# Vision tower on one core: probabilities of the first attention divided as rows, gate and value products merged, the loops of the later stages written out, the second tile's work placed sooner, and useless products on TensorE in the first microseconds

## The reference, cut to what matters

```python
x = patches(images) @ W.T + b          # 32 images, 36 patches of 768 numbers -> 256
x = concat(cls, x) + pos               # with a second class token: S = 38 rows an image
# L0 attention: 16 heads of 16, RoPE on q and k
p = softmax(where(causal, -inf, q @ k.T / 4)); x = x + (p @ v) @ Wo.T
# L0 ffn: 8 experts, the two best of each row
g = gates(top_k(x @ w_gate.T, 2)); x = x + sum_e g[:, e] * (x @ w_in[e].T @ w_out[e].T)
# L1 attention: layer norm, 16 heads, but 8 value heads; every head reads all 8 and mixes them
s = softmax(q @ k.T / 4); out = s @ v                       # (image, row, head, 8, 16)
comp = softmax(concat(qv, out) @ Ws.T + bs, over the 8); out = (comp * out).sum(over the 8)
x = x + out @ Wf.T + bf; x = x + relu(ln(x) @ Wr1.T) @ Wr2.T
# L1 ffn: ternary weights, 256 -> 1024 -> gelu -> layer norm -> 256
```

## Time and profile before

| | us |
|---|---|
| median of 3 runs | 561.5 (561.31 to 562.29) |
| the profiled execution, its own time | 560.32 |
| its span in the trace | 558.5 |
| TensorE busy in it | 506.9 |
| VectorE busy | 375.7 |
| ScalarE busy | 272.9 |
| GpSimd busy | 190.3 |

### The profile page before, as it was taken

One profiled execution on the slowest core, in us unless ns is written; L12 is line 12 of the kernel. 1 busy time (PEld: TensorE's weight loads), 2 busy tenths in 40 slices (PEclk: granted clock), 3 DMA queues, 4 the chain that ended last, 5 costly groups with the idle time before them and its releaser, 6 DMA issues.

```text
span 558.5 us, 12004 instructions
## 1 busy us (share of the span) xinstructions
PE 506.9 (91%) x3850; PEld 424.5 (76%) x3850; DVE 375.7 (67%) x943; ACT 272.9 (49%) x634; POOL 190.3 (34%) x257
## 2 busy tenths in 40 slices
PE   2969999999999887789999999999999989889996
PEld 2758878878787665567778888888888778668885
DVE  4554464555466667565997878878878787648874
ACT  3021213232331363547668777777777886434332
POOL 3320321322323311375463364364363311222230
PEclk9788899999999999999999999999999999979999
DMA  8741333243140500000000000000000000000000
GB/s 318 285 175 38 141 150 120 80 175 150 31 169 0 179 2 2 0 1 2 1 1 2 2 0 0 0 0 0 0 0 0 2 0 1 2 9 21 21 18 22
DMA packets 8685, 29.60 MB, mean 53 GB/s; under 512 B 1936, under 2 KB 3152, under 8 KB 6352
## 3 DMA queue, kind: packets, MB, share of 16 engines
q1 hardware_dynamic: 8656, 29.23, 14.4%
HBM read 27.98 MB, written 1.25 MB: 52 GB/s over the span
## 4 chain that ended last, share of the span: by engine, by line
PE 42%; DVE 5%; issue 5%; ACT 3%; POOL 1%; DVEq 1%; POOLq 0%; ACTq 0%
PE score L2051 6%; PE tb L1803 3%; PE score L1868 3%; PE bz L2081 3%; PE tb L1805 3%; PE tb L1804 3%; PE bank L1805 3%; PE bank L1804 3%; PE bank L1803 3%; PE tb L1886 2%; PE bz L2063 2%; PE bz L1817 2%; PE bz L1803 1%; DVE we_h L1433 1%; PE tb L1817 1%
## 5 line engine op out<-in xcount | busy, mean ns | idle before, releaser
L378 POOL TENSOR_TENSOR h<-h,scaled 114x256 f32 (+1 forms) x88 | 69.0, 784 | 49.3 <-ACT scaled L681 42.7
L330 POOL TENSOR_TENSOR small<-small,half 114x1 f32<-114x1 f32 x44 | 25.7, 584 | 139.4 <-DVE small L964 139.3
L547 ACT ACTIVATE p_exp<-sc,cst 114x608 f32<-114x608 f32 x66 | 48.1, 794 | 24.7 <-DVE sc L1045 24.7
L1915 PE MATMUL bz<-ebuf 128*128 128x256 f32 x256 | 58.9, 383 | 0.0
L1915 PEld LDWEIGHTS bz<-ebuf 128*128 128x128 f32 x256 | 47.8, 192 | 6.0 <-issue 0.2
L1886 PE MATMUL tb<-cst,p_exp 114*114 114x114 f32 x352 | 44.0, 266 | 9.0 <-ACT p_exp L547 3.4
L555 ACT ACTIVATE pt<-tb 114x456 f32<-114x456 f32 x66 | 34.6, 556 | 35.3 <-PE tb L1886 35.3
L2051 PE MATMUL score<-v,pt 114*114 114x137 f32 x352 | 48.9, 282 | 0.3 <-ACT o L648 0.3
L1886 PEld LDWEIGHTS tb<-cst,p_exp 114*114 114x114 f32 x352 | 35.2, 134 | 18.2 <-ACT pt L555 6.7
L681 ACT ACTIVATE scaled<-bank,gl 114x256 f32<-114x256 f32 x88 | 39.0, 473 | 17.3 <-DVE gl L1249 5.9
L2051 PEld LDWEIGHTS score<-v,pt 114*114 114x114 f32 x352 | 44.1, 178 | 2.1 <-issue 0.4
(11 more groups left out here) (216 smaller groups left out, 1338.7 us busy)
## 6 DMA issues: line engine op xcount, KB each, us to landing
ebuf<-in_w_in SPq DMA_DIRECT2D x8, 1024.0 KB, 4.8
ebuf<-in_w_out SPq DMA_DIRECT2D x8, 1024.0 KB, 6.8
x_raw<-in_x_tiles SPq DMA_DIRECT2D x11, 342.0 KB, 3.0
out<-h SPq DMA_DIRECT2D x10, 114.0 KB
raw<-in_w_a SPq DMA_DIRECT2D x4, 256.0 KB, 4.2
ebuf<-in_fc SPq DMA_DIRECT2D x1, 1024.0 KB, 5.6
ebuf<-in_proj SPq DMA_DIRECT2D x1, 1024.0 KB, 7.6
raw<-in_w_a SPq DMA_DIRECT2D x2, 384.0 KB, 5.2
```

The costliest lines, as they stand in the source:

```text
L378: gp.tensor_tensor(h[0:R, t, :], h[0:R, t, :], scaled[0:R, e % 4, :], ALU.add).then_inc(moe_acc, 1)
L547: act.activation(p_exp[0:R, :, b * S:(b + 1) * S], sc[0:R], ACT.Exp, bias=cst[0:R, CB + b:CB + b + 1], scale=SCALE).then_inc(exps, 1)
L1915: last = pe.matmul(bz[:, m * D:(m + 1) * D], ebuf[:, 0, c * D + m * P:c * D + (m + 1) * P], ebuf[:, 1, c * D:(c + 1) * D], start=(c == 0), ...
```

## The change

1. **Softmax of the first attention.** ScalarE takes the exp once, on the narrow `sc` of 608 columns. VectorE sums it over the 38 keys, takes the reciprocal of the 114 x 16 sums and multiplies `sc` by it (`a2_norm`). Three copies on ScalarE with a scale of 0 or 1 a row (`inside`) make the wide `p_exp` (`a2_wide`). The eight products with `hsum` and the wide reciprocal and product fall away, and the next `scores` waits for `xtl` instead of L1064.
2. **Products of stage C.** The gate's six passes become four, since `wc`'s two halves are taken as 16 columns for the high half of x. The products for q, k, v and the mixing, cut 512 + 152 columns before, are cut 392 + 272. The copy of the rows `qk_rows` is made in two halves, and the turns of q and k wait for both.
3. **Loops of C and D.** Both are written out in a new order on every engine, with work of stage D placed among the last turns of stage C. The loop of stage A stays. In it, half of `combine(t, 1)` now stands ahead of `a1_turn(t - 1)`.
4. **Prologue.** The second tile's patches, layer norm and products stand ahead of the preparation of the weights and of the first expert's second half.
5. **Useless products.** `warm(12)` ahead of the first tile's patches and `warm(14)` behind them multiply a matrix of ones on TensorE into a PSUM bank that is overwritten later.

```diff
+WQ = D + VW + RK
+W4 = 2 * D + W2
+C_QK, C_G, C_F, C_R1, C_R2, C_END = np.cumsum([0, DC * W4, DC * E, DC * D, DC * 2 * D, 4 * D]).tolist()
...
+            def a2_exp(n):
+                act.wait_ge(shifted, 2 * n + 2)
+                act.activation(sc[0:R], sc[0:R], ACT.Exp, scale=SCALE).then_inc(dense, 1)
+
+            def a2_wide(n, batches=range(G)):
+                act.wait_ge(scaled_rows, n + 1)
+                since(act, pt_mm, 4 * n)
+                for b in batches:
+                    act.activation(p_exp[0:R, :, b * S:(b + 1) * S], sc[0:R], ACT.Copy,
+                                   scale=inside[0:R, b:b + 1]).then_inc(exps, 1)
+
             def a2_o(t):
-                act.wait_ge(o_ready, t + 1)
+                act.wait_ge(pv0_mm, t + 1)
                 since(act, wo_mm, t)
-                act.activation(xth[1][:], y2[:], ACT.Copy).then_inc(oT_hi, 1)
+                act.activation(xth[1][:], two(score[:, 0, 0:2 * R]), ACT.Copy).then_inc(oT_hi, 1)
...
                 a1_x(t)
-                softmax_exp(t - 1)
+                a2_exp(t - 1)
+                a2_wide(t - 1)
...
-            def c2_rows(t):
-                act.wait_ge(qk1_mm, t + 1)
+            def c2_rows(t, parts):
                 since(act, qkT1_mm, 2 * t)
-                act.activation(qk_rows[0:R], tb[1][0:R, :], ACT.Copy).then_inc(qk1_out, 1)
+                if 0 in parts:
+                    act.wait_ge(qk1_mm, t + 1)
+                    act.activation(qk_rows[0:R, 0:D], tb[1][0:R, 0:D], ACT.Copy).then_inc(qk1_out, 1)
+                if 1 in parts:
+                    act.wait_ge(v1_mm, t + 1)
+                    act.activation(qk_rows[0:R, D:2 * D], tb[0][0:R, 0:D], ACT.Copy).then_inc(qk1_out, 1)
...
-            def a2_recip(t):
-                dve.wait_ge(pv0_mm, t + 1)
-                V.reciprocal(rinv0, score[:, 0, 2 * R:4 * R]).then_inc(rinv0_ready, 1)
-
-            def a2_o(t):
-                dve.wait_ge(rinv0_ready, t + 1)
-                since(dve, oT_lo, t)
-                V.tensor_tensor(y2[:], two(score[:, 0, 0:2 * R]), two(rinv0), ALU.mult).then_inc(o_ready, 1)
+            def a2_norm(n, k):
+                if k == 0:
+                    dve.wait_ge(dense, n + 1)
+                    V.tensor_reduce(psum_rows[0:R, 0], sc[0:R], AX, ALU.add).then_inc(summed, 1)
+                elif k == 1:
+                    dve.wait_ge(summed, n + 1)
+                    V.reciprocal(psum_rows[0:R, 1], psum_rows[0:R, 0]).then_inc(inverted, 1)
+                else:
+                    dve.wait_ge(inverted, n + 1)
+                    V.tensor_tensor(sc[0:R], sc[0:R], psum_rows[0:R, 1].unsqueeze(2).broadcast_to([R, H, S]),
+                                    ALU.mult).then_inc(scaled_rows, 1)
 
             def a2_lo(t):
                 dve.wait_ge(oT_hi, t + 1)
-                V.tensor_tensor(xtl[1][:], y2[:], xth[1][:].bitcast(F32), ALU.subtract).then_inc(oT_lo, 1)
+                V.tensor_tensor(xtl[1][:], two(score[:, 0, 0:2 * R]), xth[1][:].bitcast(F32), ALU.subtract).then_inc(oT_lo, 1)
...
                 softmax_max(t - 1)
                 softmax_sub(t - 1)
                 a1_x(t)
+                a2_norm(t - 1, 0)
+                a2_norm(t - 1, 1)
+                a2_norm(t - 1, 2)
                 a1_rope(t)
                 a1_pt(t - 1, (1, 3))
                 expert_lo(t)
-                a2_recip(t - 1)
-                a2_o(t - 1)
...
-            expert_lo(0)
-            prep_products()
             a1_moments(1)
-            a1_pt(0, (1, 3))
+            a2_norm(0, 0)
+            a2_norm(0, 1)
+            a2_norm(0, 2)
             a1_normed(1)
             a1_x(1)
-            a2_recip(0)
-            a2_o(0)
+            a1_pt(0, (1, 3))
+            expert_lo(0)
             a1_rope(1)
             a2_lo(0)
             a1_k(1, (0, 1))
+            prep_products()
+            a2_res(0)
+            prep_out()
+            a1_moments(2)
...
             def scores(n, causal):
                 if causal:
-                    since(pe, o_ready, n)
+                    since(pe, oT_lo, n)
...
-                            pe.matmul(score[32 * j:32 * j + 32, 0, c * R:(c + 1) * R], v0[0:R, m, e * 2 * HD:(e + 1) * 2 * HD],
+                            last = pe.matmul(score[32 * j:32 * j + 32, 0, c * R:(c + 1) * R], v0[0:R, m, e * 2 * HD:(e + 1) * 2 * HD],
                                       pt[0:R, place(2 * m + e), :], start=(e == 0), stop=(e == 1))
-                for e in range(2):
-                    for j in range(4):
-                        last = pe.matmul(score[32 * j:32 * j + 32, 0, 2 * R:4 * R], hsum[0:R, e * 2 * HD:(e + 1) * 2 * HD],
-                                         pt[0:R, place(2 * j + e):place(2 * j + e) + HQ + 1:HQ, :], start=(e == 0), stop=(e == 1))
...
+            def warm(n):
+                for i in range(n):
+                    pe.matmul(bz[:, 0:P], ones[:], ones[:], start=True, stop=True)
+
+            pe.wait_ge(init, 2)
+            warm(12)
+            pe.wait_ge(init, 5)
             a1_patch(0)
+            warm(14)
...
+                combine(t, 1, (0, 1, 2, 3))
                 a1_turn(t - 1)
-                combine(t, 1)
+                combine(t, 1, (4, 5, 6, 7))
...
+            a1_x(1)
             a1_turn(0)
-            a1_x(1)
-            a2_pv(0)
             a1_qk(1)
             a1_v(1)
+            a2_pv(0)
             combine(1, 0)
             a1_qT(1)
             a1_kT(1)
-            combine(1, 1)
-            a1_patch(2)
-            prep_qv()
             pe.wait_ge(wa_lo, 6)
             a2_wo(0)
+            prep_qv()
+            a1_patch(2)
+            combine(1, 1)
...
-                product(bk[0][0:R, 256:256 + E], xth[0], xtl[0], wc, C_G, E, (0, E)).then_inc(gate_mm, 1)
+                for c in range(DC):
+                    pe.matmul(bk[0][0:R, 256:256 + 2 * E].rearrange("p (a e) -> p a e", a=2), xth[0][:, c, :],
+                              wc[:, :, C_G + c * E:C_G + (c + 1) * E], start=(c == 0), stop=False)
+                    last = pe.matmul(bk[0][0:R, 256:256 + E], xtl[0][:, c, :], wc[:, 0, C_G + c * E:C_G + (c + 1) * E],
+                                     start=False, stop=(c == DC - 1))
+                last.then_inc(gate_mm, 1)
...
             def c2_qk(t):
                 pe.wait_ge(t2["lo"], t + 1)
-                product(tb[1][0:R, :], xth[1], xtl[1], wc, C_QK, 2 * D, (0, 2 * D)).then_inc(qk1_mm, 1)
+                since(pe, pt_odd, 2 * (t + T))
+                product(tb[1][0:R, 0:WQ], xth[1], xtl[1], wc, C_QK, W4, (0, WQ)).then_inc(qk1_mm, 1)
 
             def c2_v(t):
-                pe.wait_ge(q_ready, 2 * (t + T) + 2)
-                product(tb[0][0:R, 2 * R:2 * R + W2], xth[1], xtl[1], wc, C_V, W2, (0, W2)).then_inc(v1_mm, 1)
+                pe.wait_ge(t2["lo"], t + 1)
+                product(tb[0][0:R, 0:D + H], xth[1], xtl[1], wc, C_QK, W4, (WQ, W4)).then_inc(v1_mm, 1)
 
             def c2_qT(t):
-                pe.wait_ge(qk1_out, t + 1)
+                pe.wait_ge(qk1_out, 2 * t + 2)
+                pe.wait_ge(v1_ready, 2 * t + 2)
                 turned(tb[0][:, 0:2 * R], qk_rows[:, 0:D]).then_inc(qkT1_mm, 1)
 
             def c2_kT(t):
-                pe.wait_ge(qk1_out, t + 1)
+                pe.wait_ge(qk1_out, 2 * t + 2)
+                pe.wait_ge(v1_ready, 2 * t + 1)
...
-            def c_step(i):
-                c2_x(i - 2)
-                c2_pv(i - 3, (0, 1))
...
             c3_r2(0)
-            with pe.Fori(5, T) as i:
-                c_step(i)
+            c2_pv(2, (0,))
+            c2_x(3)
+            c2_pv(2, (1,))
+            c3_att(1)
+            c1_gate(5)
+            c2_pv(2, (2, 3))
+            c3_wf(1)
+            c2_pv(2, (4, 5))
+            c2_qk(3)
...
             c3_wf(10)
-            d2_proj(0)
+            d1_x(6)
+            d1_fc(5, (0, 1))
+            d2_turn(4, (0, 1))
+            d2_proj(3)
```

1855 lines of the change are left out of this document (1261 added, 594 removed).

## The result

The changed kernel takes 592.55 us (median of 4 runs, 589.41 to 592.97), the kernel before 561.4 (556.80 to 562.29): a ratio of 1.057 with a 95% interval of 1.051 to 1.063. The forecast was 540.5 us, and the sign was wrong. The profiled execution took 589.41 us, with a span of 587.6. Executions of one and the same kernel lie some us apart with the clock that TensorE was granted over the run: of the kernel before, beside the last experiments, one took 557.5 us at 0.990, one 564.7 at 0.969, and most 561 to 562 at 0.975.

The account below looks back on a forecast made before the run. The prediction took TensorE's work, 506.9 of 558.5 us, plus 51.6 us of its idle time as the bound. Its terms, -3.0 - 2.0 - 8.5 + 2.5 - 4.0 - 6.0, gave -21.0 and 540.5 us, range 530 to 551.

Parts of the forecast that it names:

- Start, -3.0: First tile's patches, q, k and v: useless products raise TensorE's clock, 3.0 us less of a possible 3.6.
- Prologue, -2.0: Rest of the prologue: the new order closes most of 4.2 us of TensorE idle, hsum gives 0.9; 2.0 us less.
- Loop, -8.5: Stage A's loop, six turns: 1.42 us less a turn from dropped `hsum` products and shorter waits, longer softmax chain covered.
- the 0.2 for `xn`: Stage A's loop: 0.2 us a turn gained of TensorE's 0.47 us wait for `xn`.
- the thin margin of the experts' load: Stage A's loop: 1.6 us to spare, 1.4 lost; rival that softmax or experts' weights come late, +7 us, chance 0.12.
- Bridge, +2.5: Three tiles behind stage A's loop: longer softmax chain uncovered, 0.9 us a tile, 2.5 us more in all.
- the rival of the falling clock: Bridge: TensorE less busy, so a third of its work runs at half clock, +7 to +9 us; chance 0.10.
- Gate and products, -4.0: Stage C: 0.20 us from the gate and 0.18 from re-cut products a tile, over eleven tiles, 4.0 us less.
- Tail, -6.0: Tail of stage C: stage D's work laid into TensorE's waits, against four more table loads; 6.0 us less.
- the 10.1 us: Tail of stage C: the most to gain, from 7.8 us of TensorE idle and some 2.3 of slow clock.
- The orders of C and D holding TensorE up at a place where the loop did not: Stages C and D: named as a sign that would make the forecast wrong, without size or chance.
- Faster at 0.95: Whole kernel: chance 0.95 that the change is faster, against 0.02 for same and 0.03 for slower.

Follow-up runs that it names:

- b_warm: The kernel before with the 26 useless products alone: 556.91 us, 0.995 of the kernel before.
- a_tern: The changed kernel with the absolute sum of the first ternary weight back behind tile 8's copies on ScalarE: 582.24 us, 1.041 of the kernel before.
- a_cent: The changed kernel, absolute sum and expert 1's second half-combination moved back, stage D's last product waiting only for the read of its bank: 559.4 us, 0.997.
- a_tab: a_keep with two Gelus of stage D moved behind the Exps next to them, four table loads instead of eight: 545.83 us, 0.974 of the kernel before.
- b_unroll: The kernel before with the loops of stages C and D written out on all engines, order untouched: 556.32 us, 0.992.
- a_keep: a_cent with 8, 12 and 16 useless products ahead of the turns of tiles 8, 9 and 10 in the bridge: 552.87 us, 0.986 of the kernel before.
- b_gate: The kernel before with the gate's product in four passes instead of six, parts summed by VectorE: 558.38 us, 0.997.

## Why the prediction was wrong

**Start, -3.0.** Right: 3.04 at tile 0, and 4.2 at the end in b_warm. The 18 passes of the first patches take 2.6 us (6.50 to 9.09) and not 2.1, with gaps between groups of them. A pass of 256 columns starts 0.12 behind the one before, the number I worked with, though by the rows I named for it (2144 columns in 1.16 us) it would have been 0.14.

**Prologue, -2.0.** The step that failed is "most of this idle closes, and the preparation meets new waits for VectorE". I followed TensorE's idle time and did not ask when the experts' buffer comes free. The combination that frees it had moved behind three steps, and its load is the longest wait of the stage. What it did was +1.9 by tile 1 and +3.9 in the first turn (in a_tern, with the same order, 0.4 and 5.3); mended, -4.3 beyond the start by tile 1, more than the whole term.

**Loop, -8.5.** The working of the chain held (8.9 us against 9.3, no wait at the turn). A turn gained 0.80, not 1.42: the 0.2 for `xn` did not come, and the thin margin of the experts' load, which I had as 0.2 us and put into a rival, was some 0.3 short. The six turns would have been -4.8.

**Bridge, +2.5.** Wrong by mechanism and by size. First, the forecast did not see L680 at the head of ScalarE's queue: 10.3 us. I had compared the orders of TensorE there and of ScalarE in the tail only. Second, the rest. "No combination is there to cover anything" was right, and 0.9 us a tile was about right (0.6). But I counted three tiles; tile 10's own way to C0 is a fourth, at 3.1. And the rival of the falling clock, at 0.10 and +7 to +9, is what happened: +5.5, measured by keeping it up. With the late step mended, the 12.1 us in a_cent are its clock and the 6.7 of the chain.

**Gate and products, -4.0.** The gate gave 2.7 by its median, but a turn of the full loop did not get shorter by the 0.20 that I had read off the starts of the passes; "where it is full (126.00 of 126.00) all of it counts" failed, since that loop was paced by ScalarE's exps too, 6.09 us behind the scores before and after. The re-cut was priced as passes alone (0.18 a tile); "costs nothing as long as the products of the experts stand between; they do in the new order" is the sentence that failed. The turns of q and k wait for it, by up to 0.8 us in the new order and for more in the old (2.08 at most). What the shorter passes give by themselves no run shows.

**Tail, -6.0.** The step that failed is the written-out D, which I had read as a loop without gaps. Its last product waits for a step of VectorE that the new order has late: 11.6 us. "The orders of C and D holding TensorE up at a place where the loop did not" stood in the text as what would make it wrong, without a price or a chance. It should have been a rival. The loads were close: I had left 4.1 of the 10.1 us to four loads of 5.1, and the stretch that holds them gave 5.5 when four were spared (a_tab). But the 10.1 did not close either: in the changed kernel TensorE is idle 18.8 us behind C10, where I had asked for under 4 from 424 on.

**The drain.** By the rule of the Trainium skill ("ScalarE: Activation LUTs", section "What ACT_TABLE_LOAD costs") a switch costs some 2.66 us with its drain. The rows show no drain here either, 1.28 us and the Gelu 0.01 to 0.02 behind it, and four loads spared gave 5.5 us in the stretch that holds them, 1.4 each, as estimated from two profiles. The advice of the Trainium skill in the same page's section on table sets, to do one set's work before the next, agrees with a_tab.

**The signs and the chances.** Faster at 0.95 was far too sure. Each rival changed one term of a sum that had six, and each term was a saving seen on TensorE. No rival asked what else had been put ahead of what on the other engines. With what was found mended, a_tab is at 545.8, 5 us above the forecast: of the 52 us between the changed kernel and the forecast, 21.6 went with the two late steps, 11.6 with the wait for the bank, 6.5 with the useless products in the bridge and 7.0 with the two Gelus. That it comes so near is in part luck. By the table a_tab has gained 8.1 at tile 1 (the sum: 5.0), 5.7 in the loop (8.5) and 6.3 from C0 to the end (10.0), and lost 5.5 in the bridge (2.5), with products in it that the forecast did not have.

## What to carry to other kernels

When an order is rewritten, walk every engine's queue and ask of each step that moved up what it waits for, and of each that moved down who waits for it; one step that nobody needs yet, at the head of a queue with its load still to come, cost 10 us. A wait should name the read that frees the bank and no later event. A longer chain is free only where other work covers it, and where it is bare it costs twice, by itself and through TensorE's clock. An engine that is busy all the time in a loop may still be paced by another one, so ask for the start of each product and not only for the idle time. Gains that are small and alone true (the clock at the start, the gate, the loops written out) are worth measuring alone, since a bundle hides both them and its faults.

## What the runs showed of the hardware

- A loop written out in the same order took 0.37 us less a turn where a turn is 6 us long, and nothing where it is 21 us long (b_unroll).
- Useless products kept TensorE at full clock through waits of 2 to 4 us: granted clock 0.93 and 1.00 in the two windows of the bridge, against 0.87 and 0.84, for 5.5 us of time (a_keep, a_cent).
- A table load showed 1.28 us and no drain in every row; where four were spared, the stretch that held them was 5.5 us shorter, about half of it by a higher granted clock (a_keep, a_tab).
- A loop in which the profile has TensorE busy for all of its time did not get shorter by two passes less: the matmul behind them started 0.39 us after the one before it instead of 0.23 (b_gate, before).
